# Norming the router's rows on GpSimd: the subtract-and-scale of a layer norm, moved off the vector engine

## The reference

```
x = x + ga * attention(layernorm(x) * (1 + ca) + sa)      16 heads, causal, rotary keys and queries
x = x + gb * experts(layernorm(x) * (1 + cb) + sb)
```

```
def _layernorm(x, axis=-1, eps=1e-05):
    m = jnp.mean(x, axis=axis, keepdims=True)
    v = jnp.var(x, axis=axis, keepdims=True)
    return (x - m) / jnp.sqrt(v + eps)

h = _layernorm(x) * (1 + cb) + sb
h = h @ Wm + bm ; t = 8 slices of 32 channels of each token
w = softmax(t @ expert_emb)            16 experts, the top 2 of them
out = sum over the top 2 of w_e * (gelu(t @ W1_e + b1_e) @ W2_e + b2_e)
x = x + gb * (out @ Wo + bo)
```

## Time and profile before

| | |
|---|---|
| device time, median of 3 runs | 2950.63 us (2949.89 to 2953.15) |
| span of the profiled execution, first to last instruction | 2947.5 us |
| PE busy | 2823.2 us (96%) |
| DVE busy | 1869.7 us (63%) |
| ACT busy | 1806.7 us (61%) |
| POOL busy | 1243.5 us (42%) |
| granted TensorE clock, mean | 0.991 of full speed |

### The profile page before, as it was taken

One profiled execution on the slowest core, in us unless ns is written; L12 is line 12 of the kernel. 1 busy time (PEld: TensorE's weight loads), 2 busy tenths in 40 slices (PEclk: granted clock), 3 DMA queues, 4 the chain that ended last, 5 costly groups with the idle time before them and its releaser, 6 DMA issues.

```text
span 2947.5 us, 51530 instructions
## 1 busy us (share of the span) xinstructions
PE 2823.2 (96%) x16460; PEld 1254.0 (43%) x16460; DVE 1869.7 (63%) x4636; ACT 1806.7 (61%) x2148; POOL 1243.5 (42%) x1325
## 2 busy tenths in 40 slices
PE   6789999999999999999999999999999999999999
PEld 2344444444444444444434444444444444444433
DVE  5665766756667566666666666675756657666553
ACT  1346675566755667456674576655766566655687
POOL 4311555126551364413644146531465225661254
PEclk9889999999999999999999999999999999999999
DMA  6303443034430444204432044321553124531243
GB/s 141 73 1 84 113 121 96 4 98 112 133 73 2 106 123 118 70 8 119 121 100 70 21 128 122 90 56 29 134 130 91 34 63 115 130 84 27 74 129 93
DMA packets 177556, 253.06 MB, mean 86 GB/s; under 512 B 51085, under 2 KB 83869, under 8 KB 177197
## 3 DMA queue, kind: packets, MB, share of 16 engines
q1 hardware_dynamic: 170300, 247.79, 32.9%
q10 hardware_dynamic: 6996, 1.99, 0.3%
HBM read 159.13 MB, written 12.63 MB: 58 GB/s over the span
## 4 chain that ended last, share of the span: by engine, by line
PE 85%; DVE 6%; issue 3%; ACT 2%; POOL 1%; SPq 0%; DMA 0%; ACTq 0%; DVEq 0%; POOLq 0%
PE ps L1236 17%; PE ps L1272 17%; PE ps L1290 16%; PE ps L1256 9%; PE ps L418 8%; PE ps L464 4%; PE ps L505 2%; PE ps L466 2%; PE ps L535 2%; DVE front L561 1%; PE ps L516 1%; DVE rest L1392 1%; PE ps L492 1%; PE ps L523 1%; PE ps L450 1%
## 5 line engine op out<-in xcount | busy, mean ns | idle before, releaser
L1356 ACT ACTIVATE rest<-ps 128x1024 f32<-128x1024 f32 x1024 | 993.7, 1024 | 341.2 <-PE ps L1272 341.1
L1338 ACT ACTIVATE rest<-ps 128x1024 f32<-128x1024 f32 (+3 forms) x768 | 608.6, 810 | 550.1 <-PE ps L1236 536.4
L1456 POOL TENSOR_TENSOR rest<-rest 128x512 f32<-128x512 f32 x478 | 631.9, 1322 | 560.6 <-DVE rest L1392 550.1
L1392 DVE SCALAR_TENSOR_TENSOR rest<-ps,b2c,wide 128x512 f32<-128x512 f32 x512 | 383.8, 750 | 490.4 <-PE ps L1290 460.7
L1272 PE MATMUL ps<-wide,w1s 98*128 98x512 f32 x2048 | 644.6, 434 | 11.5 <-ACT rest L1356 8.7
L1290 PE MATMUL ps<-rest,w2s 128*32 128x512 f32 x4096 | 546.1, 605 | 0.6 <-ACT rest L1356 0.6
L1446 POOL TENSOR_SCALAR_AFFINE_SELECT rest<-rest 128x256 f32<-128x256 f32 x512 | 204.3, 407 | 806.7 <-ACT rest L1338 803.6
L558 DVE CUSTOM_DVE_ANT_0 rest<-ps,maskd 128x256 f32<-128x256 f32 (+3 forms) x1024 | 458.7, 487 | 121.9 <-PE ps L418 114.6
L1236 PE MATMUL ps<-wide 49*128 49x512 f32 (+3 forms) x2304 | 485.7, 511 | 7.2 <-ACT rest L1338 6.1
L1272 PEld LDWEIGHTS ps<-wide,w1s 98*128 98x128 f32 x2048 | 346.0, 189 | 238.4 <-ACT rest L1356 109.4
L561 DVE TENSOR_REDUCE front<-ps 128x1 f32<-128x512 f32 x512 | 329.1, 685 | 103.7 <-PE ps L418 99.9
(11 more groups left out here) (138 smaller groups left out, 2225.0 us busy)
## 6 DMA issues: line engine op xcount, KB each, us to landing
wide<-gate_rows SPq DMA_DIRECT2D x1024, 128.0 KB, 2.8
wide<-front SPq DMA_DIRECT2D x480, 64.0 KB, 2.0
wide<-front SPq DMA_DIRECT2D x192, 128.0 KB, 2.4
ao<-in_x SPq DMA_DIRECT2D x16, 512.0 KB, 5.0
heads<-front SPq DMA_DIRECT2D x64, 128.0 KB, 2.4
xs<-in_x SPq DMA_DIRECT2D x16, 512.0 KB, 5.1
out<-xs SPq DMA_DIRECT2D x32, 256.0 KB, 2.7
wide<-ao SPq DMA_DIRECT2D x96, 64.0 KB, 2.3
```

The source lines that it names most:

```text
L1338: nc.scalar.activation(L.pt[:, u % PTS, :, f:HALF], L.ps[:, 2 * (u % 2):2 * (u % 2) + 2, 0:HALF - f], ACT.Exp, scale=SCALE).then_inc(S["c_ ...
L1356: nc.scalar.activation(L.hm[:, u % HM, :], bank(2 * (u % 2), 2), ACT.Gelu).then_inc(S["e_gelu"], 1)
L1392: v.scalar_tensor_tensor(out=dst, in0=bank(L2 + q % 2), scalar=L.b2c[:, e:e + 1], in1=L.gb[:, q // 2 % GB, q % 2, :], op0=ALU.add, op1=ALU ...
L1456: g.tensor_tensor(dst, dst, L.gy[:, k % GY, :], ALU.add).then_inc(S["e_add"], 1)
```

## The change

The four instructions of "xn" are issued on POOL in place of DVE, behind the same wait on the power's semaphore. Their operands, their semaphore and the item's slot stay as they are.

```diff
 def item_vector(v, L, R, item):
 
     S, kind = L.S, item[0]
-    if kind in READER or kind == "exp":
+    if kind in READER or kind in ("exp", "xn"):
         return
@@
-    elif kind == "xn":
-        c = item[1]
-        v.wait_ge(S[f"d{c}_rs"], 1)
-        for t in range(4):
-            v.tensor_scalar(L.xn2[:, t, :], L.xs[:, 4 * c + t, :], L.tmv[:, t, 0:1], L.tstd[:, t:t + 1], ALU.subtract,
-                            ALU.mult).then_inc(S[f"d{c}_xn"], 1)
@@ def item_pool(g, L, R, item):
         g.tensor_tensor(L.tstd[:, :], L.tvar[:, :], L.mhalf[:, 0:4], ALU.pow).then_inc(S[f"d{c}_rs"], 1)
+    elif kind == "xn":
+        c = item[1]
+        g.wait_ge(S[f"d{c}_rs"], 1)
+        for t in range(4):
+            g.tensor_scalar(L.xn2[:, t, :], L.xs[:, 4 * c + t, :], L.tmv[:, t, 0:1], L.tstd[:, t:t + 1], ALU.subtract,
+                            ALU.mult).then_inc(S[f"d{c}_xn"], 1)
```

## The result

The changed kernel takes 2978.06 us (median of 4 runs, 2974.47 to 2983.08) against 2950.26 us in the runs beside it: a ratio of 1.0093, 95% interval 1.0078 to 1.0109. It is slower by 28 us. The prediction said 2948.6 us, with a range to 2962 us: wrong, in sign and in range. What happened is what the text had as its second rival, with a cost on top that no term of it had.

The account below looks back on a forecast made before the run. PE, busy 2823.2 of 2947.5 us, was taken as the bound. Attention, transposes and adds 0, L523's wait -2.0 us: span 2945.5, plus 3.1 us from span to median gives 2948.6 us; range 2945.5 to 2962 us.

Parts of the forecast that it names:

- second rival: Expert places: POOL becomes the bound, slower if one instruction takes over 0.86 us; 2964 to 2976 us; chance 0.20.
- The attention places cost 0: Eight attention places: the four instructions fall into POOL's idle 7.09 us before the select, cost 0 in both directions.
- The room in the expert slots is 2.45 us, T = 0.61 us: Expert places: POOL's start at 655.79 to PE's transposes at 658.30; PE waits only if one instruction exceeds 0.61 us.
- T: Time of one of the four norming instructions on POOL, start to start; taken as 0.41 to 0.5 us.
- The bound from above, 1.47 us for two passes: Upper end for one POOL instruction if its two operations cost two tensor_tensor passes; 27 us over eight expert places.
- DVE's lead removes the wait at L523: Expert places: DVE runs some 1.2 us sooner up to L597, ending PE's 0.29 us wait, 2.0 us in seven images.
- The later adds cost 0 for T up to 0.75: Expert places: POOL's third to fifth adds move later, but POOL catches up before the next image's power; cost 0.
- rival 2: The second rival: POOL becomes the bound at the expert places, 2964 us at 1.1 us an instruction; chance 0.20.

Follow-up runs that it names:

- att_only: Changed kernel with only the attention half normed on POOL, the expert half on DVE as before: ratio 0.9995, interval 0.9983 to 1.0007.
- att_double: Changed kernel with POOL doing four more such instructions into spare tiles ahead of the attention half's four: first to last power 2586.7 us, the changed kernel's to a tenth.
- exp_two: Changed kernel, but in the expert slots POOL norms tiles 0 and 1 only, DVE tiles 2 and 3: ratio 1.0001.
- forms: Changed kernel with POOL's four attention-half instructions made four kinds (as before, subtract alone, constants, half the columns): 1.226, 0.929, 1.078, 0.799 us each; no whole time given.
- early_xn: Changed kernel with POOL's expert-half norming moved from slot 7 to slot 5, ahead of two adds: ratio 1.0089, interval 1.0070 to 1.0108.
- exp_three: Changed kernel, but in the expert slots POOL norms tiles 0 to 2 and DVE tile 3: ratio 1.0018, interval 1.0005 to 1.0031.
- exp_only: Changed kernel with only the expert half normed on POOL, the attention half on DVE as before: ratio 1.0072, interval 1.0057 to 1.0088.
- filled: Changed kernel with PE doing nine more matmuls of 512 columns while it waits in the expert slots: 2971.49 us, ratio 1.0059.

## Why the prediction was wrong

By its steps:

1. *The attention places cost 0.* Right. `att_only` is the kernel before, and `att_double` shows that twice the load would have been free too.
2. *The room in the expert slots is 2.45 us, T = 0.61 us.* Nearly right: by the waits it is some 2.6 us (two tiles of 2.62 us in all do not wait, three of 3.67 us wait 1.07 us, four of 4.84 us wait 2.25 us). POOL starts the four 3.69 us behind the power's start, where the text had 3.84: an add waits for the sum of the add before and starts 0.14 us behind its end, and the four, which wait for no add, follow the second add at once. The row of L511 also names this wait as the text said.
3. *T is 0.41 to 0.5 us.* **This step failed.** It is 1.226 us (1.21 start to start). I took the affine select's price because shape and inputs agree; but on POOL the price is one of the kind of instruction. By the two sizes of the select in the trace before, 0.407 us for 256 elements and 0.282 for 128, it costs 0.98 ns an element; a tensor_tensor costs 2.1, and this one 3.3 (the row of the smaller select, in the groups of POOL before, stands below this list). (The text also spoke of three columns of scalars; the instruction has two.) The bound from above, 1.47 us for two passes, held; the middle way would have been the safer choice, since two of the three priced kinds on POOL (the add and the power) spoke for over 0.7 us. Of the two figures of the Trainium skill (GPSIMD Engine Reference, section 3.1), the rate of 1.03 cycles an element would have misled further: 3.3 ns an element are 4.0 cycles at 1.2 GHz, its clock there (section 1). Its factor of two against VectorE, measured there on a tensor_tensor, gives T = 0.82 and would have been nearer than my price; measured here is a factor of 3.0. The measurement decides.
4. *DVE's lead removes the wait at L523, 2.0 us, and no other.* Right, to the row: the row is gone in the changed kernel and in `exp_two`, and the others are as before. In the changed kernel it is hidden under the loss; alone it is 1.8 us in seven images (`exp_two`, in which one wait of 0.3 us is counted against it). Nor does POOL's norming hinder DVE's passes, as the text said: a gating pass takes 0.751 us in the median before and after, and at most 0.753 and 0.755.
5. *The later adds cost 0 for T up to 0.75.* Right, and still at 1.21: POOL's three adds end at 669.84, and the power follows at 670.41 behind DVE.
6. *Slower from T = 0.86 on (rival 2).* The mechanism and place are right. What was missing is the clock: with T = 1.21, 4 x 1.21 - 2.45 = 2.39 us x 8 less 2.0 gives +17, where the trace gives 18.0 - 2.0 = +16 and four half-clock stretches of 1.45 us, +5.8. Their sum, 21.8, is what the span shows behind the opening (24.8 less 3.3 is 21.5). No term of my sum had the clock. The trace before shows full clock (1.00) from image 1 to the last power, but it had a sign behind it that I overlooked: in the last image PE waits 2.55 us for ACT, and 2 us later the clock is at half for 3.4 us and the matmuls are slow (rows below this list). In `att_only` the same wait of 2.55 us has no such stretch behind it (1.00 there), so this too comes at some places and not at others. The chance of 0.20 for this rival, and a range that ended at T = 1.04, were too small for a price that no row showed.

```profile
2831.99 0.74 PE L1272 MATMUL ps<-wide,w1s 98*128 98x512 f32 x2 [2.55 <-ACT rest L1356]
2833.57 1.65 PE L1290 MATMUL ps<-rest,w2s 128*32 128x512 f32 x8
...
2834.00:2837.30 3.30, 3.30 (x16) 1.31 (x12) 2.89 (x4) 1.59 (x2) 1.54 (x2) 0.50 0.84 233
```

```profile
L971 POOL TENSOR_SCALAR_AFFINE_SELECT ident<-ident 128x128 f32<-128x128 f32 x1 | 0.3, 282 | 0.0
```

Against the median the account is: 27.8 us measured, 21.5 in the profiled execution behind the opening, and the remaining 6 are the opening (3.3 in the profiled executions) and the runs' scatter (the profiled execution is the fastest of the four).

Is there a version that beats both? `exp_two` has 1.8 us in seven images over the kernel before, and its whole time (1.0001, 0.9989 to 1.0013) cannot show it. I would not claim more.

## What to carry to other kernels

A price on GpSimd belongs to the kind of instruction, not to its shape: before moving work there, measure that very instruction in a place where nobody waits (as `forms` did), since kinds differ by more than three times an element. Then compare the sum with the room at the consumer, tile by tile; here the same four instructions were free where the engine was idle for 7 us, and made the kernel 28 us slower where some 2.6 us were left; two of the four there cost nothing. Where the bounding engine is made to wait, look at its granted clock too: here that was a quarter of the loss. And an engine with 63% busy is no reason to unload it when the table of waits of the bounding engine does not name the work.

## What the runs showed of the hardware

- TensorE's granted clock fell to 1.2 GHz behind idle waits of 2.25 us at four of eight places in the changed kernel, behind waits of 1.76 to 1.81 us at six of seven places in `early_xn`, and behind none of the eight waits of 1.07 us in `exp_three`. One such stretch cost about 1.45 us on top of the wait. The places repeated: the same four in the changed kernel's two profiles, in `att_double` and in `forms`, but another four in `exp_only`. With PE kept busy in the wait (`filled`) there was none.
- GpSimd's tensor_scalar with two operations and two columns of scalars, float32: 1.226 us for 128x256, 0.799 us for 128x128; with constants 1.078 us; with the subtract alone 0.929 us. VectorE does the first in 0.409 us when undisturbed. Beside one of VectorE's of the same kind, GpSimd's first took 1.42 us (`exp_two`), and VectorE's took up to 1.50 us beside GpSimd's adds.
